# A graph-network kernel: gathered rows added by the DMA instead of VectorE, and DMA issues moved between queues

## The chip, the cores and the metric

The kernel runs on one core of a Trainium2 chip. The metric is the device time of one execution in microseconds (us). In what follows PE is the matrix engine (TensorE), DVE is VectorE, ACT is ScalarE, POOL is GpSimd, and SP is the sync engine, which only issues DMAs here. Several engines can issue DMAs: SP and ACT through hardware queues, POOL through a software queue.

## The reference

There are 12,500 nodes with 64 features each and 400,000 edges, sorted by target node `dst`. One attention-like graph layer comes first, then three message-passing layers with shared edges, with a residual and a layer norm after each of the two parts. The message-passing layer is the part that matters here:

```python
def _gnn_layer(nf, traj, src, dst, We, be, Wn, bn):
    ef = jnp.concatenate([nf[src], nf[dst], traj[:, None]], axis=-1)
    msg = jax.nn.leaky_relu(ef @ We.T + be, negative_slope=0.01)
    red = jax.ops.segment_sum(msg, dst, num_segments=nf.shape[0])
    h = jnp.concatenate([nf, red], axis=-1)
    return jax.nn.leaky_relu(h @ Wn.T + bn, negative_slope=0.01)

x = _layernorm(x + _L0_gnn_ref(x, L0_gnn_Wh, L0_gnn_weight, src, dst), axis=-1)
x = _layernorm(x + _L1_gnn_ref(x, edge_weight, src, dst, ...three layers...), axis=-1)
```

## The kernel before

`We` is split, so that the message of an edge is `leaky(A[src] + B[dst] + traj * w)`, with `A` and `B` projected once per node and layer into the tables `tabs[:, 0]` and `tabs[:, 1]`. A one-time part sorts and lays out the edges. Then the program goes through four rounds (`number` 0 to 3: the attention layer and the three message layers). Each round has a source stage, a target stage and a short dense part (`between`), and every engine waits for the end of a stage before it goes on.

**Source stage** (`source_phase`, 960 groups of 512 edges, in the order of source nodes). For each group ACT copies the table rows of one window of 128 nodes to a buffer (`window`, line 1329; the window number is loaded from `win_s` into a register). PE multiplies them with 0/1 matrices in fp8 (`hits_s`, made by DVE in round 0 and loaded by SP, line 1292, in the others), four blocks of 128 edges, three bf16 pieces each (line 1355), plus one matmul a block for the edge weight (line 1350, from `side`, line 1295; line 1352 in round 0). That is 16 matmuls a group, into one PSUM bank. DVE copies the bank to `made` (line 1378). Two groups are a lot; ACT issues the store of a lot to the table `rows` in HBM (line 1322). There are four windows, four banks, four `made` buffers; all the waits are semaphore counts (`s_window`, `s_rows`, `s_read`, `s_in`, `s_out`).

**Target stage** (`target_phase`, 976 groups, worked in 488 pairs, in the order of target nodes; rounds 1 to 3). POOL gathers 128 rows of 1 KB for each group by an indirect DMA (line 1563) into `quads`. ACT copies the window of `B` rows (line 1588); PE spreads them over the edges of the group into the PSUM bank `z` with 12 matmuls (`before_message`, line 1604; its 0/1 matrices `hits_g` come by SP, line 1573). DVE then works on a pair at a time, 512 columns on 128 partitions: `add` (line 1636: PSUM `z` plus `quads` to `msg`), `leaky` (line 1640), and `less` and `split` (lines 1644 and 1648), which cut the fp32 message into three bf16 pieces. PE sums the messages per target node (`scatter`, line 1408 in the helper `scatter_pieces`, 12 matmuls a group), two pairs behind `before_message`, and DVE adds each group's sum to `hr` (`keep`, line 1655). The order on DVE is written out for each pair `p`: `add(p)`, `less(p-1)`, `leaky(p)`, `split(p-1)`, and the two `keep` of pair `p-3`. Loops on ACT, SP and PE run in laps of 8 groups (`laps`); the lists of POOL and DVE are unrolled.

The target stage of round 0 (`first_target_phase`) gathers in the same way (line 1439) and is not touched.

Of the kernel before, what the change touches and what calls it, by code (L numbers as in the profile page):

```python
# [36 lines left out]
SLOTS = 512  # L37
# [50 lines left out]
def build(nc, x, src, dst, edge_weight, w_head, w_out, w_edge, b_edge, w_traj, w_node, b_node, out):  # L88
# [1135 lines left out]
    def laps(engine, count, step):  # L1224

        for q in range(LAP):
            step(q, q, 0)
        with engine.Fori(1, count // LAP - 1) as i:
            for q in range(LAP):
                step(i * LAP + q, q, i)  # L1230
        for g in range(count - LAP, count):
            step(g, g % LAP, g // LAP)
# [24 lines left out]
    def source_phase(number, ready, table, width):  # L1257

        layered = number > 0
        s_in, s_out = ([sem_of(f"rows_{what}{n}", layered) for n in range(4)] for what in ("in", "out"))  # L1260
        s_window, s_rows, s_read = (sem_of("rows_" + what, layered) for what in ("window", "rows", "read"))
# [4 lines left out]
        since, since_in, since_out = past * NS, past * (NS // LAP) * 32, past * (NS // LAP) * 16  # L1266
# [4 lines left out]
        window = [room.cut(3 * D // 2, BF16) for _ in range(4)]  # L1271
# [12 lines left out]
        def _(syn):  # L1284
            def load(l, n):
# [9 lines left out]
                syn.dma_start(side[0:high - low, n % 4, :, :], meta[at, low:high, :].rearrange("g r s -> r g s")).then_inc(s_in[n % 4], 16)  # L1295
# [16 lines left out]
            laps(syn, NS, step)  # L1312
            if not layered:
                store_hits(lots - 1, lots - 1)

        @block.scalar
        def _(sca):
            def store(l, n):
                if isinstance(l, int) and l < 0:
                    return  # L1320
                sca.wait_ge(s_read, since + (l + 1) * GROUP_LOT)
                sca.dma_start(to_rows[:, bass.ds(l * GROUP_LOT, GROUP_LOT), :], made[n % 4]).then_inc(s_out[n % 4], 16)
# [9 lines left out]
            for l in range(lots - 2, lots):  # L1332
                store(l, l)
# [718 lines left out]
```

## Time and profile before

| | us |
|---|---|
| median of 3 runs | 13956.04 (13951.84 to 13956.06) |
| the profiled execution, its own time | 13966.42 |
| span of the profiled execution | 13965.2 |
| source stage, round 0 | 3491 to 4555 (1064) |
| target stage, round 0 | 4590 to 5970 (1380) |
| source stages, rounds 1, 2, 3 | 955, 983, 982 |
| target stages, rounds 1, 2, 3 | 1531, 1535, 1537 |

The stage times are read from the first and last instruction of the lines that only this stage runs. The busy shares over the span are 66% for PE, 78% for DVE, 40% for ACT and 33% for POOL. These are averages over stages with different limits, so the stage tables and the waits have to be read stage by stage. In the rows further down, "PE" and "PEld" are the matmuls and the weight loads, whose ends are modelled; the number in brackets at the end of a timeline row is the idle time of the engine before it and what ended that.

### The profile page before, as it was taken

The page shows a single profiled execution, that of the slowest core. Times are in us where ns is not written, and L with a number is a line of the kernel's source. Part 1 is how long each engine was busy: PE and PEld are TensorE (multiplying, and loading weights), DVE is VectorE, ACT ScalarE, POOL GpSimd, SP SyncE. Part 2 cuts the span into 40 slices and gives each one's busy share as a digit, 9 for nine tenths or more (in the row PEclk, how much of TensorE's full clock was granted, in tenths as well). Part 3 has the DMA queues.
Part 4 walks back from the last instruction along what each step waited for, and adds up shares of the span by engine and source line. Part 5 has one row for each costly group of instructions (what it writes and reads, how often), then busy time and mean ns, then how long its engine had stood idle before and what let it go on. Part 6 is the DMA issues. An engine that isn't in the chain of part 4 may idle for free. (4 is left out here: it accounts for less than half of the span.)

```text
span 13965.2 us, 514377 instructions
## 1 busy us (share of the span) xinstructions
PE 9172.6 (66%) x172644; PEld 7604.8 (54%) x172644; DVE 10842.4 (78%) x26542; ACT 5627.0 (40%) x15578; POOL 4548.9 (33%) x4413
## 2 busy tenths in 40 slices
PE   6777777762777666667766556666555566666566
PEld 4555555541666555556655554555555555555554
DVE  8999999964777899854479996445999854479997
ACT  4666666630333688743322222333222233322222
POOL 0000000047000677610056663001666600046664
PEclk9999999965555788768899998999999989999997
DMA  1000000011788666746655555666555646665555
GB/s 34 5 5 6 5 5 6 3 25 30 238 241 241 181 197 196 172 129 207 207 180 172 172 171 98 201 201 195 171 171 171 161 123 201 201 188 171 172 172 111
DMA packets 1700459, 1931.56 MB, mean 138 GB/s; under 512 B 222450, under 2 KB 1571268, under 8 KB 1699460
## 3 DMA queue, kind: packets, MB, share of 16 engines
q1 hardware_dynamic: 977585, 893.89, 22.1%
q0 software_dynamic: 199680, 520.06, 15.1%
q10 hardware_dynamic: 522544, 510.34, 10.4%
q8 instruction: 238, 3.90, 0.1%
q14 instruction: 412, 3.38, 0.1%
HBM read 1202.74 MB, written 725.45 MB: 138 GB/s over the span
## 5 line engine op out<-in xcount | busy, mean ns | idle before, releaser
L1563 POOL DMA_INDIRECT work<-rows,quad_at x2928 | 3091.0, 1056 | 4501.8 <-DMA rows<-work 2007.4
L1378 DVE COPY work<-bank 128x256 f32<-128x256 f32 (+1 forms) x3840 | 1630.7, 425 | 1773.0 <-PE bank L1355 1748.6
L1408 PE MATMUL bank<-work 128*128 128x64 bf16 x46848 | 2077.6, 199 | 1361.4 <-DVE hr L1655 1352.2
L1355 PE MATMUL bank<-work 128*128 128x64 bf16 x46080 | 2726.2, 211 | 0.0
L1408 PEld LDWEIGHTS bank<-work 128*128 128x128 fp8e4 (+1 forms) x46848 | 1848.9, 102 | 1517.7 <-issue 1464.9
L1329 ACT COPY work<-tabs 128x192 bf16 x3840 | 1348.9, 351 | 2819.9 <-PE bank L1355 1579.4
L1588 ACT COPY work<-tabs 128x192 bf16 x2928 | 1028.9, 351 | 3548.4 <-PE bank L1604 3242.2
L1355 PEld LDWEIGHTS bank<-work 128*128 128x128 fp8e4 x46080 | 2394.1, 109 | 0.0
L1350 PE MATMUL bank<-wtraj,side 128*128 128x64 bf16 x11520 | 1772.3, 205 | 925.1 <-ACT work L1329 657.8
L521 ACT ACTIVATE work<-work,tabs 128x128 bf16<-128x128 bf16 x6250 | 1919.2, 427 | 935.0 <-DVE work L721 935.0
L1350 PEld LDWEIGHTS bank<-wtraj,side 128*128 128x128 bf16 x11520 | 1194.0, 104 | 1237.4 <-DVE work L1378 580.1
L1604 PE MATMUL bank<-work 128*128 128x64 bf16 x35136 | 1311.1, 196 | 521.1 <-DMA work<-hits_g 291.6
L1604 PEld LDWEIGHTS bank<-work 128*128 128x128 fp8e4 x35136 | 1173.8, 100 | 651.7 <-issue 600.6
L602 PE MATMUL bank<-work 128*128 128x384 bf16 x9375 | 1294.6, 292 | 40.5 <-ACT work L521 40.5
L725 DVE TENSOR_TENSOR work<-work,tabs 128x768 bf16<-128x768 bf16 x2500 | 1223.9, 552 | 0.0
L1439 POOL DMA_INDIRECT work<-rows,quad_at x976 | 986.8, 1011 | 410.1 <-issue 208.3
L1636 DVE TENSOR_TENSOR work<-bank,work 128x512 f32<-128x512 f32 x1464 | 1012.8, 692 | 129.9 <-PE bank L1604 100.4
L602 PEld LDWEIGHTS bank<-work 128*128 128x128 bf16 x9375 | 826.6, 102 | 389.0 <-issue 61.0
L1640 DVE SCALAR_TENSOR_TENSOR work<-work 128x512 f32<-128x512 f32 x1464 | 1002.8, 685 | 0.1
L1648 DVE TENSOR_TENSOR work<-work 128x512 bf16<-128x512 f32 x1464 | 1002.4, 685 | 0.1
L1644 DVE TENSOR_TENSOR work<-work 128x512 f32<-128x512 f32 x1464 | 998.1, 682 | 0.0
L1352 PE MATMUL bank<-ones_b,side 128*128 128x1 bf16 x3840 | 719.8, 190 | 411.7 <-DVE work L1370 239.4
(323 smaller groups left out, 12309.8 us busy)
## 6 DMA issues: line engine op xcount, KB each, us to landing
work<-hits_g SPq DMA_DIRECT2D x1464, 256.0 KB, 2.7
rows<-work ACTq DMA_DIRECT2D x1440, 256.0 KB, 2.1
work<-hits_s SPq DMA_DIRECT2D x1440, 128.0 KB
hits_g<-work SPq DMA_DIRECT2D x976, 128.0 KB
rows<-work ACTq DMA_DIRECT2D x480, 260.0 KB, 4.6
work<-rows,quad_at POOLq DMA_INDIRECT x3904
work<-meta_src SPq DMA_DIRECT2D x480, 128.0 KB
hits_s<-work SPq DMA_DIRECT2D x480, 128.0 KB, 4.2
```

Of the source, the lines that this page charges most:

```text
L521: last = sca.activation(values[lot % 3][:, f, j // 2, :, j % 2], of_tile(hit_col[lot % 3], j), ACT.Copy, scale=of[name][:, t:t + 1])
L602: last = ten.matmul(to[:, f * P:3 * P].rearrange("p (f c) -> p f c", c=P), of_tile(hit_row[lot % 3], j), v[:, fields[0]:fields[1], j // 2, ...
L725: last = vec.tensor_tensor(values[at][:, f, :, :, :], hit_col[at], twos(lot, name, P), ALU.mult)
L1329: sca.copy(window[q % 4].unsqueeze(1), tabs[:, 0, bass.ds(w, 1), :]).then_inc(s_window, 1)
L1350: ten.matmul(home, beside, wtraj[:, :], start=True, stop=False, skip_group_check=True)
L1355: last = ten.matmul(home, hits[n][:, q % GROUP_LOT, slots], window[q % 4][:, k * D:(k + 1) * D], start=False, stop=k == 2, skip_group_chec ...
L1378: vec.tensor_copy(made[n][:, q % GROUP_LOT, :], bank[q % 4][:, 0:QUAD * width]).then_inc(s_read, 1)
L1408: last = ten.matmul(to[:, 0:D], hits_of(j), piece_of(j), start=j == 0 and k == 0, stop=j == QUAD - 1 and k == 2, skip_group_check=True)
L1563: pool.indirect_dma_start(quads[g // 2 % (GATHERED // 2)][:, half(g)], None, table, bass.IndirectOffsetOnAxis(ap=quad_at[:, g:g + 1], axis ...
L1588: sca.copy(window[q % 4].unsqueeze(1), tabs[:, 1, bass.ds(w, 1), :]).then_inc(s_window, 1)
L1604: last = ten.matmul(to[:, j * D:(j + 1) * D], hits_t[:, j * P:(j + 1) * P], window[q % 4][:, k * D:(k + 1) * D], start=k == 0, stop=k == 2 ...
L1636: vec.tensor_tensor(msg[p % 4], z[p % 4][:, :], quads[p % (GATHERED // 2)], ALU.add).then_inc(s_added, 1)
```

## The change

In the source stage, the store of a lot goes from ACT to SP, and the load of `side` goes from SP to POOL, each lot with its own semaphore (`s_side`). There are eight windows and eight PSUM banks instead of four. This applies to all four rounds.

In the target stage, ACT copies `z` of a pair from PSUM to one of eight `msg` buffers (`hold`), one pair behind its window copies. POOL's indirect DMA no longer writes into `quads`: it adds its rows onto `msg` (`compute_op=ALU.add`). DVE's `add` is gone, and `leaky` waits for the gathers directly. `scatter` runs five pairs behind `before_message` instead of two; `hits_g` has eight buffers; the loops run in laps of 16 groups. The order on DVE becomes `leaky(p)`, `keep`, `less(p)`, `keep`, `split(p)`.

```diff
-    def laps(engine, count, step):
-        for q in range(LAP):
+    def laps(engine, count, step, size=LAP):
+        for q in range(size):
...
-        since, since_in, since_out = past * NS, past * (NS // LAP) * 32, past * (NS // LAP) * 16
+        since, since_in, since_out = past * NS, past * (NS // LAP) * 16, past * (NS // LAP) * 16
...
-        window = [room.cut(3 * D // 2, BF16) for _ in range(4)]
+        window = [room.cut(3 * D // 2, BF16) for _ in range(8)]
...
-                syn.dma_start(side[0:high - low, n % 4, :, :], meta[at, low:high, :].rearrange("g r s -> r g s")).then_inc(s_in[n % 4], 16)
+            def store(l, n):
+                if isinstance(l, int) and l < 0:
+                    return
+                syn.wait_ge(s_read, since + (l + 1) * GROUP_LOT)
+                syn.dma_start(to_rows[:, bass.ds(l * GROUP_LOT, GROUP_LOT), :], made[n % 4]).then_inc(s_out[n % 4], 16)
...
                     load(l + 3, q // GROUP_LOT + 3)
+                    store(l - 2, q // GROUP_LOT + 2)
                     if not layered:
                         store_hits(l - 1, q // GROUP_LOT + 3)
...
+        @block.gpsimd
+        def _(pool):
+            def load_side(l, n):
+                if isinstance(l, int) and l >= lots:
+                    return
+                at_least(pool, s_rows, (l - 4) * GROUP_LOT + GROUP_LOT, since)
+                pool.dma_start(side[0:high - low, n % 4, :, :], meta[bass.ds(l * GROUP_LOT, GROUP_LOT), low:high, :].rearrange(
+                    "g r s -> r g s")).then_inc(s_side[n % 4], 16)
+            def step(g, q, lap):
+                if q % GROUP_LOT == 0:
+                    load_side(lap * (LAP // GROUP_LOT) + q // GROUP_LOT + 3, q // GROUP_LOT + 3)
+            for l in range(3):
+                load_side(l, l)
+            laps(pool, NS, step)
         @block.scalar
...
             def step(g, q, lap):
-                if q % GROUP_LOT == 0:
-                    store(lap * (LAP // GROUP_LOT) + q // GROUP_LOT - 2, q // GROUP_LOT + 2)
                 w = register(sca, win_s[0:1, bass.ds(g, 1)], NW - 1)
-                at_least(sca, s_rows, g - 3, since)
-                sca.copy(window[q % 4].unsqueeze(1), tabs[:, 0, bass.ds(w, 1), :]).then_inc(s_window, 1)
+                at_least(sca, s_rows, g - 7, since)
+                sca.copy(window[q % 8].unsqueeze(1), tabs[:, 0, bass.ds(w, 1), :]).then_inc(s_window, 1)
...
-                ten.wait_ge(s_in[n], since_in + (lap + 1) * 32)
-                if not layered:
+                ten.wait_ge(s_side[n], since_in + (lap + 1) * 16)
+                if layered:
+                    ten.wait_ge(s_in[n], since_in + (lap + 1) * 16)
+                else:
                     ten.wait_ge(s_hits, g + 1)
-                at_least(ten, s_read, g - 3, since)
-                to = bank[q % 4]
+                at_least(ten, s_read, g - 7, since)
+                to = bank[q % 8]
...
+        AROUND, BEHIND = 8, 5
+        lap_groups = 2 * AROUND
         s_quads = [sem_of(f"sums_quads{n}", True) for n in range(GATHERED)]
...
-        quads = [room.cut(2 * QUAD * D) for _ in range(GATHERED // 2)]
-        hits_home = [room.cut(SLOTS, BF16).rearrange("p (g c) -> p g c", g=2) for _ in range(4)]
+        hits_home = [room.cut(SLOTS, BF16).rearrange("p (g c) -> p g c", g=2) for _ in range(AROUND)]
         window = [room.cut(3 * D // 2, BF16) for _ in range(4)]
-        msg, rest = ([room.cut(2 * QUAD * D) for _ in range(4)] for _ in range(2))
+        msg = [room.cut(2 * QUAD * D) for _ in range(AROUND)]
+        rest = [room.cut(2 * QUAD * D) for _ in range(4)]
...
             for g in range(NG):
-                at_least(pool, s_added, (g - GATHERED) // 2 + 1, since_pairs)
-                pool.indirect_dma_start(quads[g // 2 % (GATHERED // 2)][:, half(g)], None, table,
-                                        bass.IndirectOffsetOnAxis(ap=quad_at[:, g:g + 1], axis=0)).then_inc(s_quads[g % GATHERED], 16)
+                if g % 2 == 0:
+                    pool.wait_ge(s_held, since_pairs + g // 2 + 1)
+                at_least(pool, s_leaky, (g - GATHERED) // 2 + 1, since_pairs)
+                pool.indirect_dma_start(msg[g // 2 % AROUND][:, half(g)], None, table,
+                                        bass.IndirectOffsetOnAxis(ap=quad_at[:, g:g + 1], axis=0),
+                                        compute_op=ALU.add).then_inc(s_quads[g % GATHERED], 16)
...
-                at_least(syn, s_sum, 2 * (p - 3), since)
-                syn.dma_start(hits_home[n % 4], hits_g[bass.ds(p * 2, 2), :, :].rearrange("g p c -> p g c")).then_inc(s_in[n % 4], 16)
+                at_least(syn, s_sum, 2 * (p - AROUND + 1), since)
+                syn.dma_start(hits_home[n % AROUND], hits_g[bass.ds(p * 2, 2), :, :].rearrange("g p c -> p g c")).then_inc(
+                    s_in[n % AROUND], 16)
...
+            def hold(p, n):
+                sca.wait_ge(s_before, since + 2 * (p + 1))
+                at_least(sca, s_sum, 2 * (p - AROUND + 1), since)
+                sca.copy(msg[n], z[n % 4][:, :]).then_inc(s_held, 1)
             def step(g, q, lap):
                 w = register(sca, win_g[0:1, bass.ds(g, 1)], NW - 1)
                 at_least(sca, s_before, g - 3, since)
                 sca.copy(window[q % 4].unsqueeze(1), tabs[:, 1, bass.ds(w, 1), :]).then_inc(s_window, 1)
-            laps(sca, NG, step)
+                if q % 2 == 1 and (not isinstance(g, int) or g >= 2):
+                    hold(lap * AROUND + (q // 2 - 1), (q // 2 - 1) % AROUND)
+            laps(sca, NG, step, lap_groups)
+            hold(pairs - 1, (pairs - 1) % AROUND)
...
                 if q % 2 == 0:
-                    at_least(ten, s_added, lap * (LAP // 2) + (q // 2 - 3), since_pairs)
+                    at_least(ten, s_held, lap * AROUND + (q // 2 - 3), since_pairs)
                 settle(ten, "tensor", g)
-                to = z[q // 2][:, half(q)]
+                to = z[q // 2 % 4][:, half(q)]
...
-                if q % 2 == 1 and (not isinstance(g, int) or g >= 4):
-                    for h in (5, 4):
-                        scatter(g - h, (q - h) % LAP, lap - (q < h))
-            laps(ten, NG, step)
-            for g in range(NG - 4, NG):
-                scatter(g, g % LAP, g // LAP)
+                if q % 2 == 1 and (not isinstance(g, int) or g >= 2 * BEHIND):
+                    for h in (2 * BEHIND + 1, 2 * BEHIND):
+                        scatter(g - h, (q - h) % lap_groups, lap - (q < h))
...
-            def add(p):
-                vec.wait_ge(s_before, since + 2 * (p + 1))
+            def leaky(p):
                 for g in (2 * p, 2 * p + 1):
                     vec.wait_ge(s_quads[g % GATHERED], since_quads + 16 * (g // GATHERED + 1))
-                at_least(vec, s_sum, 2 * (p - 3), since)
-                vec.tensor_tensor(msg[p % 4], z[p % 4][:, :], quads[p % (GATHERED // 2)], ALU.add).then_inc(s_added, 1)
-            def leaky(p):
-                vec.wait_ge(s_added, since_pairs + p + 1)
-                vec.scalar_tensor_tensor(msg[p % 4], msg[p % 4], SLOPE, msg[p % 4], ALU.mult, ALU.max).then_inc(s_leaky, 1)
+                row = msg[p % AROUND]
+                vec.scalar_tensor_tensor(row, row, SLOPE, row, ALU.mult, ALU.max).then_inc(s_leaky, 1)
             def less(p):
                 vec.wait_ge(s_leaky, since_pairs + p + 1)
-                vec.tensor_tensor(rest[p % 4], msg[p % 4], upper(msg[p % 4]), ALU.subtract).then_inc(s_rest, 1)
+                at_least(vec, s_sum, 2 * (p - 3), since)
+                vec.tensor_tensor(rest[p % 4], msg[p % AROUND], upper(msg[p % AROUND]), ALU.subtract).then_inc(s_rest, 1)
...
             for p in range(pairs + 3):
                 if p < pairs:
-                    add(p)
-                if 1 <= p <= pairs:
-                    less(p - 1)
-                if p < pairs:
                     leaky(p)
-                if 1 <= p <= pairs:
-                    split(p - 1)
                 if p >= 3:
                     keep(2 * p - 6)
+                if p < pairs:
+                    less(p)
+                if p >= 3:
                     keep(2 * p - 5)
+                if p < pairs:
+                    split(p)
```

## Rows read from the trace of the kernel before

**Rows 1.** The page's costliest groups: the two gathers of POOL.

```profile
L1563 POOL DMA_INDIRECT work<-rows,quad_at x2928 | 3091.0, 1056 | 4501.8 <-DMA rows<-work 2007.4
...
L1439 POOL DMA_INDIRECT work<-rows,quad_at x976 | 986.8, 1011 | 410.1 <-issue 208.3
```

**Rows 2.** Busy time by stage: stretch, length, each engine, granted clock, DMA share, GB/s.

```profile
3491.00:4555.00 1064.00, 829.75 (x15360) 737.29 (x15360) 761.31 (x1919) 337.23 (x960) 0.00 (x0) 0.51 0.81 240
...
6102.00:7057.00 955.00, 691.92 (x15354) 592.53 (x15355) 407.06 (x959) 337.21 (x960) 0.00 (x0) 0.87 0.64 206
7061.00:8592.00 1531.00, 908.40 (x23424) 812.75 (x23424) 1382.32 (x2927) 342.59 (x975) 1029.49 (x976) 0.97 0.61 168
...
8706.00:9689.00 983.00, 663.33 (x15360) 556.53 (x15360) 407.29 (x959) 337.22 (x960) 0.00 (x0) 0.92 0.62 201
9693.00:11228.00 1535.00, 907.47 (x23424) 812.19 (x23424) 1382.39 (x2927) 342.98 (x976) 1030.90 (x976) 0.96 0.61 167
...
11340.00:12322.00 982.00, 661.54 (x15346) 556.27 (x15347) 406.82 (x959) 337.23 (x960) 0.00 (x0) 0.92 0.62 201
12326.00:13863.00 1537.00, 913.10 (x23424) 816.87 (x23424) 1381.92 (x2928) 342.81 (x976) 1030.62 (x976) 0.96 0.61 169
```

**Rows 3.** Timeline of DVE in the target stage of round 1, one pair: start, length.

```profile
7301.72 0.69 DVE L1636 TENSOR_TENSOR work<-bank,work 128x512 f32<-128x512 f32 x1
7302.33 0.68 DVE L1644 TENSOR_TENSOR work<-work 128x512 f32<-128x512 f32 x1
...
7304.13 0.21 DVE L1655 TENSOR_TENSOR hr<-hr,bank 128x64 f32 x1
...
7304.77 0.69 DVE L1636 TENSOR_TENSOR work<-bank,work 128x512 f32<-128x512 f32 x1
```

**Rows 4.** Timeline of POOL over the same pair.

```profile
7301.09 0.95 POOL L1563 DMA_INDIRECT work<-rows,quad_at  x1 [0.30 <-issue]
7302.68 1.16 POOL L1563 DMA_INDIRECT work<-rows,quad_at  x1 [0.64 <-DVE work L1636]
7304.14 0.96 POOL L1563 DMA_INDIRECT work<-rows,quad_at  x1 [0.30 <-issue]
```

**Rows 5.** Waits in the target stage of round 1 (7100 to 8550): total, times, longest.

```profile
POOL work L1563 <- DVE work L1636: 322.3, 467, 3.0
```

**Rows 6.** Timeline of ACT in the source stage of round 2, one lot.

```profile
9301.94 0.35 ACT L1329 COPY work<-tabs 128x192 bf16 x1 [0.85 <-PE bank L1355]
9302.74 0.35 ACT L1329 COPY work<-tabs 128x192 bf16 x1 [0.45 <-issue]
9302.97 0.38 ACTq L1322 DMA_DIRECT2D rows<-work  x1
9303.93 0.35 ACT L1329 COPY work<-tabs 128x192 bf16 x1 [0.84 <-PE bank L1355]
```

**Rows 7.** Waits of PE in the source stage of round 2 (8800 to 9600).

```profile
PE bank L1350 <- ACT work L1329: 188.6, 333, 1.1
```

**Rows 8.** Waits of SP's queue in the same stretch.

```profile
SPq L1292 <- PE bank L1355: 347.8, 390, 1.9
```

**Rows 9.** DMA queues and issues in the target stage of round 1 (7100 to 8550): share of 16 engines.

```profile
q0 software_dynamic: 44710, 122.17, 31.4%
q1 hardware_dynamic: 126741, 122.18, 29.2%
...
work<-hits_g SPq DMA_DIRECT2D x467, 256.0 KB, 2.7
work<-rows,quad_at POOLq DMA_INDIRECT x933
```

**Rows 10.** Groups of ACT by shape: a PSUM copy of 128x512 in the dense part.

```profile
L1775 ACT COPY work<-bank 128x512 f32<-128x512 f32 x72 | 41.9, 581 | 53.4 <-PE bank L1769 53.4
```

**Rows 11.** Timeline of ACT in the target stage of round 2: the second window copy of a pair.

```profile
9903.14 0.35 ACT L1588 COPY work<-tabs 128x192 bf16 x1 [0.22 <-issue]
```

**Rows 12.** Timeline of PE in the target stage of round 1: 24 matmuls early and late in it.

```profile
7072.25 1.47 PE L1604 MATMUL bank<-work 128*128 128x64 bf16 x24
...
8000.49 0.86 PE L1604 MATMUL bank<-work 128*128 128x64 bf16 x24
```

More of the change, by code:

```diff
@@ L1222, in build @@
     LAP = 8
-    def laps(engine, count, step):
-        for q in range(LAP):
+    def laps(engine, count, step, size=LAP):
+        for q in range(size):
             step(q, q, 0)
[L1228 to L1232, printed above, removed]
+        with engine.Fori(1, count // size - 1) as i:
+            for q in range(size):
+                step(i * size + q, q, i)
+        for g in range(count - size, count):
+            step(g, g % size, g // size)
     serial = itertools.count()
@@ L1260, in source_phase @@
         s_in, s_out = ([sem_of(f"rows_{what}{n}", layered) for n in range(4)] for what in ("in", "out"))
+        s_side = [sem_of(f"rows_side{n}", layered) for n in range(4)]
         s_window, s_rows, s_read = (sem_of("rows_" + what, layered) for what in ("window", "rows", "read"))
@@ L1312, in _ @@
             laps(syn, NS, step)
+            for l in range(lots - 2, lots):
+                store(l, l)
             if not layered:
                 store_hits(lots - 1, lots - 1)
+        @block.gpsimd
[12 more added lines that the diff above has]
+            laps(pool, NS, step)
         @block.scalar
         def _(sca):
[L1318 to L1322, printed above, removed]
             def step(g, q, lap):
-                if q % GROUP_LOT == 0:
-                    store(lap * (LAP // GROUP_LOT) + q // GROUP_LOT - 2, q // GROUP_LOT + 2)
                 w = register(sca, win_s[0:1, bass.ds(g, 1)], NW - 1)
-                at_least(sca, s_rows, g - 3, since)
-                sca.copy(window[q % 4].unsqueeze(1), tabs[:, 0, bass.ds(w, 1), :]).then_inc(s_window, 1)
+                at_least(sca, s_rows, g - 7, since)
+                sca.copy(window[q % 8].unsqueeze(1), tabs[:, 0, bass.ds(w, 1), :]).then_inc(s_window, 1)
             laps(sca, NS, step)
-            for l in range(lots - 2, lots):
-                store(l, l)
         @block.tensor
@@ L1354, in step @@
                     for k in range(3):
-                        last = ten.matmul(home, hits[n][:, q % GROUP_LOT, slots], window[q % 4][:, k * D:(k + 1) * D], start=False,
+                        last = ten.matmul(home, hits[n][:, q % GROUP_LOT, slots], window[q % 8][:, k * D:(k + 1) * D], start=False,
                                           stop=k == 2, skip_group_check=True)
@@ L1377, in read @@
                     at_least(vec, s_out[n], lap * 16, since_out)
-                vec.tensor_copy(made[n][:, q % GROUP_LOT, :], bank[q % 4][:, 0:QUAD * width]).then_inc(s_read, 1)
+                vec.tensor_copy(made[n][:, q % GROUP_LOT, :], bank[q % 8][:, 0:QUAD * width]).then_inc(s_read, 1)
             def step(g, q, lap):
@@ L1535, in target_phase @@
     def target_phase(number, stored, ready, table):
+        AROUND, BEHIND = 8, 5
+        lap_groups = 2 * AROUND
         s_quads = [sem_of(f"sums_quads{n}", True) for n in range(GATHERED)]
[L1538 to L1540 removed]
+        s_in = [sem_of(f"sums_in{n}", True) for n in range(AROUND)]
+        s_window, s_before, s_held, s_leaky, s_rest, s_split, s_sum, s_kept = (sem_of("sums_" + what, True) for what in (
+            "window", "before", "held", "leaky", "rest", "split", "sum", "kept"))
         past = number - 1
         pairs = NG // 2
[L1544 removed]
+        since, since_pairs, since_quads = past * NG, past * pairs, past * (NG // GATHERED) * 16
+        since_in = past * (pairs // AROUND) * 16
         room = Room(work, WORK - NG)
[L1546 to L1547 removed]
+        hits_home = [room.cut(SLOTS, BF16).rearrange("p (g c) -> p g c", g=2) for _ in range(AROUND)]
         window = [room.cut(3 * D // 2, BF16) for _ in range(4)]
[L1549 removed]
+        msg = [room.cut(2 * QUAD * D) for _ in range(AROUND)]
+        rest = [room.cut(2 * QUAD * D) for _ in range(4)]
         low = [room.cut(QUAD * D, BF16) for _ in range(4)]
```

20 lines of the change are left out of this document (10 added, 10 removed).

## The prediction

> **What bounds the kernel now.** I read the page's costliest groups first, then the busy times cut at the stage borders, and then the waits and a few microseconds of timeline inside each stage that the diff touches. The median is 13956.0; the profiled execution took 13966.4, 10 more, and its span is 13965.2. The sum below is made on the profiled execution and 10 is taken off at the end.
>
> The three layered target stages take 1531, 1535 and 1537, together 4603. DVE is busy for 1382 of each [rows 2], and its timeline shows why nothing else sets their pace: in the steady state operation follows operation. The 512-column operations start 0.60 to 0.61 apart, the two `keep` take 0.64 from the start of the first to the next `add`, and a pair repeats after 3.05 [rows 3]. Over the whole stage it is 1531/488 = 3.14 a pair, 1.03 times the steady figure, for the start and some irregular pairs. POOL gives two gathers a pair, and the first of them waits for DVE's `add` [rows 4, 5]: POOL is held back and is not the limit. PE is busy for 0.59 of the stage, the DMA engines for 0.61 [rows 2].
>
> The source stages of rounds 1 to 3 take 955, 983 and 982, or 0.995 and 1.02 a group. No engine is near full: PE 0.72 at most, ACT 0.35, DMA 0.64 [rows 2]. ACT's timeline shows a fixed beat of 2.0 a lot: 0.80 from the first window copy to the second, then a DMA issue, and the next copy 0.96 after that issue began [rows 6]. Of the 0.80, 0.35 is the copy and 0.45 is "issue", ACT's own register load and address work. PE waits for ACT's window [rows 7]. So ACT's instruction stream sets this stage, though ACT is busy for a third of it.
>
> The source stage of round 0 takes 1064, or 1.108 a group, with the DMA share at 0.81 and the PE clock at the lower of its two levels, 0.51 of 2.4 GHz [rows 2].
>
> **Target stage, part by part.** DVE loses `add` and nothing comes in its place: three operations at 0.60 and two `keep` at 0.20 is 2.20 a pair. The two `keep` used to stand side by side and the second waits for the first; in the new order a long operation lies between, so 0.20 each is what 0.64 leaves without that wait, an estimate from their length of 0.21. DVE's floor is 2.20, so another engine must take over.
>
> ACT gains one PSUM copy of 128x512, 0.58 in the dense part [rows 10]. Two window copies at 0.35+0.22 [rows 11] and the hold at 0.58+0.22 are 1.94 a pair. That is under every pace below, so it lies beside other work. If POOL and DVE both went under 1.94 it would be the price.
>
> PE does the same 48 matmuls a pair: 24 take 0.86 at the upper clock and 1.47 at the lower one [rows 12], so 1.7 or 2.94. The granted clock in these stages is 0.96 to 0.97 [rows 2], and a shorter pair leaves PE fewer idle gaps, so I take 1.7, hidden.
>
> POOL: a gather occupies it for 0.95 to 1.16 and 0.30 more lies between two [rows 4]; the mean is 1.056 [rows 1]. Nothing in this trace adds in a DMA, so its price is bounded. From below: a gather costs what it does at best, 0.96+0.30 = 1.26, a pair 2.52. From above: both sides of the transfer cost again, a busy time of 2.11, a pair 4.82. The longer gathers here are those beside DVE operations with two SBUF inputs [rows 3, 4], and in the new order three of five DVE operations are of that kind, so I don't take 1.26. With the mean, a pair is 2 x (1.056+0.30) = 2.71, and with the factor 1.03 of the present stage 2.79. I take this: the number of rows and addresses that POOL handles for one gather is unchanged. The first gather of a pair now waits for `hold` instead of `add`; behind it in POOL's queue are only later gathers, and ACT holds a pair up to four banks ahead, so this wait should be short.
>
> The Trainium skill ("GPSIMD Engine Reference", When to use GPSIMD) says that one of a pair of POOL's cores writes the read descriptors and another the write descriptors. If an adding transfer needs two reads for each row, the reading core would have twice the descriptors; that speaks against this change, and no row here shows how the 0.96 is divided. By the rule taken literally a pair would be near the 4.82.
>
> DMA engines: the gathers take 0.314 of 1450 for 933, 0.49 each of all 16 engines, and `hits_g` 0.292 of 1450 for 467, 0.91 a pair [rows 9]. A pair now asks for 1.88. An adding gather also reads 128 KB of SBUF: at nothing a pair still asks for 1.88; at double 2 x 0.98 + 0.91 = 2.87. The highest share in any row is 0.81 [rows 2], so the pace that DMA allows is 1.88/0.81 = 2.3 to 2.87/0.81 = 3.5. It reaches POOL's 2.79 when an adding gather costs 1.4 times a plain one. I take it as just hidden, between the ends.
>
> The Trainium skill ("Collectives: The Full Stack", The bandwidth ceiling) says that an adding DMA is slower because it needs two source reads on the same queue, measured at 32.35 against 62.28 GB/s, a ratio of 1.93. By that figure a pair would ask for 2 x 0.94 + 0.91 = 2.8, and 3.46 at a share of 0.81. No run so far shows it on this kernel.
>
> Depth: `scatter` five pairs behind gives a gather about four pairs, 11, for hold, queue and landing, so latency should not bind. The drain at the end is three pairs longer; with the start I add 15. A stage is 488 x 2.79 + 15 = 1377. It saves 154 + 158 + 160 = 472. Bounds: 488 x 2.52 + 15 = 1245 (saves 868) and 488 x 4.82 + 15 = 2367 (costs 2498).
>
> **Source stage, part by part.** ACT loses the store, its wait for `s_read` and its issue. What remains is the 0.80 between two copies with no DMA issue between them [rows 6]; in the target stage the same sequence takes 0.57 [rows 11], the lower bound. DMA asks for 0.62 x 1.024 = 0.64 a group, at a share of 0.81 that is 0.79. PE needs 16 x 0.86/24 = 0.57 at the upper clock and 0.98 at the lower. I take 0.80, because two independent rows meet there: 960 x 0.80 = 768. It saves 187 + 215 + 214 = 616. Bounds: DMA at full share, 0.64 or 614 (saves 1078); and nothing saved.
>
> SP gets the store (0.38 of issue [rows 6]) and loses `side`. It idles 0.89 a lot now [rows 8]. What is queued behind the new wait for `s_read` is the next lot's `hits_s` load, three lots ahead, so a short wait costs nothing; if the store came late, `made` (four buffers) would stop DVE and then PE. POOL gets the 480 `side` loads a stage; no plain DMA from POOL is in the trace, and even at the longest gather here, 1.16+0.30 [rows 4], it fits in a lot of 1.6. POOL has no other work there, so it is hidden; if it landed over three lots late, PE would stand. Eight windows and banks remove waits that are small beside ACT's beat.
>
> Round 0 asks for 0.81 x 1.108 = 0.90 of DMA a group already near the highest share, on the lower PE clock. I take 25 saved, between 100 (1.00 a group) and 40 lost, since three large DMAs of a lot now stand in SP's queue.
>
> **Sum.** 13966 - 472 - 616 - 25 = 12853, less 10 for the median: about 12845.
>
> **The rivals.**
>
> (a) The forecast: POOL paces the target stage near 2.8 and the source stage goes to 0.8. 12845, chance 0.44.
>
> (b) DMA paces the target stage, because an addition reads twice. For it: hits and gathers already take 0.61 of the engines. Against it: the 0.49 a gather may be mostly HBM latency. A pair of 2.87 to 3.53, in the middle 3.2: 488 x 3.2 + 15 = 1577, 128 more than now in three stages, with the source gain of 641 it is 13443 (ends 12950 and 13925). Chance 0.22.
>
> (c) The other side: POOL needs clearly longer to issue an adding gather. It decides from a pair of 3.55, where the three target stages lose the 641 that the source stages save: divided by 1.03, 3.45 a pair, 1.42 busy for a gather instead of 1.056. At double it is 13956 + 2498 - 641 = 15813. For it: an added read for each row is more to describe. Against it: the rows and addresses are the same in number. Chance 0.15.
>
> (d) The source stage gains nothing, since SP's store or POOL's `side` takes the place of ACT's issue, while the target stage goes as forecast: 13956 - 472 = 13484. SP's idle time speaks against it. Chance 0.13.
>
> (e) Both parts go better, 2.52 a pair and 0.72 a group (saves 868, 847, 60): 12180. Chance 0.06.
>
> **How the numbers follow.** 0.2%, 28, is about what can be told from no change. Range 12200 to 13950: it holds (a), (b), (d) and most of (e), and leaves out (c). The likeliest case alone is 12500 to 13100. Faster: 0.44 + 0.20 + 0.12 + 0.06 = 0.82; same, from the edges of (b) and (d): 0.03; slower, (c): 0.15.
>
> **What would show it.** POOL's gather row: about 1.06 says (a), over 1.4 says (c). DMA queue q0 over 0.7 a gather with POOL waiting for `leaky` says (b). ACT's two window copies at about 0.8 with no DMA issue between, and PE waiting less for ACT, show the source step; a stage still at 955 to 983, with DVE waiting for `rows` stores or PE for `side`, says (d). The prediction is wrong mainly if the addition's price, which no row shows, is far from that of a plain gather.

## The result and the profile after

The changed kernel takes 14252.2 us (median of 4 runs, 14246.3 to 14269.9) against 13955.8: the ratio is 1.0215, 95% interval 1.0197 to 1.0233. It is slower by 2.0% to 2.3%, where 8% faster was forecast, and it lies outside the range. The profiled execution has a span of 14246.8. In the sessions of three kernels further down (moved_only, side_on_pool, plain_half_rows) the kernel before itself took 15367 and 15396, with long waits inside the target stages that the profile names "remote", so of these three only ratios, differences from that kernel, the lengths of source stages and the least length of an instruction are used.

Busy time by stage in the changed kernel, with the same columns as [rows 2]:

```profile
3487.00:4537.00 1050.00, 773.24 (x15360) 707.66 (x15360) 740.57 (x1920) 337.12 (x960) 280.44 (x480) 0.57 0.85 243
6082.00:6815.00 733.00, 559.64 (x15360) 493.07 (x15360) 378.36 (x960) 337.33 (x960) 263.26 (x480) 0.99 0.87 269
6820.00:8680.00 1860.00, 1169.53 (x23424) 1065.72 (x23424) 1070.50 (x2440) 606.47 (x1464) 1549.76 (x976) 0.69 0.75 138
8793.00:9549.00 756.00, 571.92 (x15360) 498.72 (x15360) 386.27 (x960) 337.30 (x960) 263.26 (x480) 0.99 0.85 261
9553.00:11409.00 1856.00, 1155.04 (x23424) 1052.16 (x23424) 1069.97 (x2440) 622.39 (x1464) 1544.79 (x976) 0.71 0.76 138
11521.00:12273.00 752.00, 574.32 (x15360) 499.89 (x15360) 384.49 (x960) 337.34 (x960) 263.26 (x480) 0.99 0.85 262
12278.00:14145.00 1867.00, 1171.74 (x23424) 1067.14 (x23424) 1073.04 (x2439) 622.29 (x1464) 1549.26 (x976) 0.69 0.75 139
```

Two large effects of opposite sign stand in this table. The layered source stages fell from 955, 983 and 982 to 733, 756 and 752: 679 saved. Round 0 saved 14. The target stages rose from 1531, 1535 and 1537 to 1860, 1856 and 1867: 980 lost. Together that is 287 more, and the spans differ by 282.

The page's two gathers, as in [rows 1]:

```profile
L1586 POOL DMA_INDIRECT work<-rows,quad_at x2928 | 4643.8, 1586 | 944.1 <-issue 837.6
...
L1457 POOL DMA_INDIRECT work<-rows,quad_at x976 | 985.4, 1010 | 410.8 <-PE bank L1426 209.1
```

In the mean, the adding gather takes POOL 1.586 instead of 1.056, and the plain one of round 0 is unchanged at 1.01. POOL over one pair (as [rows 4]):

```profile
7301.99 1.55 POOL L1586 DMA_INDIRECT work<-rows,quad_at  x1 [0.30 <-issue]
7303.85 1.55 POOL L1586 DMA_INDIRECT work<-rows,quad_at  x1 [0.30 <-issue]
7305.70 1.55 POOL L1586 DMA_INDIRECT work<-rows,quad_at  x1 [0.30 <-issue]
```

The gathers follow each other with only the 0.30 that lies between any two. A pair takes 3.70 here and (1.586+0.30) x 2 = 3.77 in the mean, and 488 of them are 1840 of the stage's 1860. DVE in the same microseconds (as [rows 3]), and the waits of that stage from 6900 to 8600 (as [rows 5]):

```profile
7302.50 0.69 DVE L1669 SCALAR_TENSOR_TENSOR work<-work 128x512 f32<-128x512 f32 x1 [1.64 <-DMA work<-rows,quad_at]
7303.11 0.21 DVE L1685 TENSOR_TENSOR hr<-hr,bank 128x64 f32 x1
7303.24 0.68 DVE L1674 TENSOR_TENSOR work<-work 128x512 f32<-128x512 f32 x1
...
7306.10 0.69 DVE L1669 SCALAR_TENSOR_TENSOR work<-work 128x512 f32<-128x512 f32 x1 [1.44 <-DMA work<-rows,quad_at]
```

```profile
DVE work L1669 <- DMA work<-rows,quad_at: 699.7, 450, 2.7
...
POOL work L1586 <- issue: 259.2, 850, 0.3
POOL work L1586 <- DVE work L1669: 8.5, 28, 0.3
```

DVE's part went as planned and bought nothing: it is done with a pair in about 2.2 and then idles 1.4 to 1.6 for the gather, 700 of 1700. POOL waits for hardly anything: the 0.30 between its gathers adds up to 259, and DVE holds it up for 8.5. The DMA queues in that stretch (as [rows 9]):

```profile
q0 software_dynamic: 129482, 117.92, 51.3%
q1 hardware_dynamic: 122344, 117.94, 24.0%
...
work<-hits_g SPq DMA_DIRECT2D x449, 256.0 KB
work<-rows,quad_at POOLq DMA_INDIRECT x900
```

A gather now takes 0.513 x 1700/900 = 0.97 of all 16 DMA engines instead of the 0.49 of the kernel before: twice as much. A pair asks for 2 x 0.97 + 0.91 = 2.85, in a pair of 3.77.

### The profile page after: what moved, and what is told of

It reads as the page before. It is cut to its first block and busy times, and to the rows that moved or that the text cites. A ratio compares the mean times of both kernels' runs of the same rounds, so it can differ in the third digit from the quotient of the medians.

```text
span 14246.8 us, 520948 instructions
## 1 busy us (share of the span) xinstructions
PE 9551.7 (67%) x172644; PEld 8089.3 (57%) x172644; DVE 9813.9 (69%) x25078; ACT 6447.6 (45%) x17042; POOL 7167.2 (50%) x6333
## 5 line engine op out<-in xcount | busy, mean ns | idle before, releaser
L1586 POOL DMA_INDIRECT work<-rows,quad_at x2928 | 4643.8, 1586 | 944.1 <-issue 837.6
L1426 PE MATMUL bank<-work 128*128 128x64 bf16 x46848 | 2553.6, 216 | 2036.8 <-DVE hr L1685 1790.4
L1426 PEld LDWEIGHTS bank<-work 128*128 128x128 fp8e4 (+1 forms) x46848 | 2207.1, 113 | 2327.3 <-issue 2255.9
L1373 PE MATMUL bank<-work 128*128 128x64 bf16 x46080 | 2403.7, 203 | 0.0
L1613 ACT COPY work<-bank 128x512 f32<-128x512 f32 x1464 | 856.6, 585 | 3239.2 <-PE bank L1637 3238.7
L1396 DVE COPY work<-bank 128x256 f32<-128x256 f32 (+1 forms) x3840 | 1553.9, 422 | 1106.3 <-DMA rows<-work 601.7
L1331 POOL DMA_DIRECT2D side<-meta x1920 | 1070.2, 558 | 2308.3 <-PE bank L1373 2098.1
L1373 PEld LDWEIGHTS bank<-work 128*128 128x128 fp8e4 x46080 | 2156.4, 104 | 0.0
L1368 PE MATMUL bank<-wtraj,side 128*128 128x64 bf16 x11520 | 1557.5, 195 | 555.3 <-ACT work L1347 247.1
L1637 PE MATMUL bank<-work 128*128 128x64 bf16 x35136 | 1784.5, 222 | 61.4 <-DMA work<-hits_g 30.5
L1637 PEld LDWEIGHTS bank<-work 128*128 128x128 fp8e4 x35136 | 1629.0, 117 | 82.0 <-issue 50.9
L1368 PEld LDWEIGHTS bank<-wtraj,side 128*128 128x128 bf16 x11520 | 1129.3, 98 | 770.0 <-DVE work L1396 508.5
L1457 POOL DMA_INDIRECT work<-rows,quad_at x976 | 985.4, 1010 | 410.8 <-PE bank L1426 209.1
```

The lines of the kernel that those rows point to most:

```text
L1331: pool.dma_start(side[0:high - low, n % 4, :, :], meta[bass.ds(l * GROUP_LOT, GROUP_LOT), low:high, :].rearrange("g r s -> r g s")).then_i ...
L1368: ten.matmul(home, beside, wtraj[:, :], start=True, stop=False, skip_group_check=True)
L1373: last = ten.matmul(home, hits[n][:, q % GROUP_LOT, slots], window[q % 8][:, k * D:(k + 1) * D], start=False, stop=k == 2, skip_group_chec ...
L1396: vec.tensor_copy(made[n][:, q % GROUP_LOT, :], bank[q % 8][:, 0:QUAD * width]).then_inc(s_read, 1)
L1426: last = ten.matmul(to[:, 0:D], hits_of(j), piece_of(j), start=j == 0 and k == 0, stop=j == QUAD - 1 and k == 2, skip_group_check=True)
L1586: pool.indirect_dma_start(msg[g // 2 % AROUND][:, half(g)], None, table, bass.IndirectOffsetOnAxis(ap=quad_at[:, g:g + 1], axis=0), comput ...
```

## The experiments

Ratios are against the kernel before, run on the same chip in the same session; apart from the three kernels named above, it took 13956 to 13977 there.

**The two parts by themselves.** tgt_only has the source stage of before and the target stage of after; src_only the reverse (each function taken whole, so the diff is the one half or the other of the change).

> Source stages as before, target stages as in the changed kernel. Theory (POOL pays for the adding gather, nothing else of the loss comes from elsewhere): source stages back to 955 to 983, target stages 1855 to 1867, so about 13956 + 979 = 14935. Rival (the two parts disturb each other, for instance through the clock or the buffers): off this sum by more than 60.

> Target stages as before, source stages as in the changed kernel. Theory (the two parts are independent): the three layered source stages save 682 and round 0 saves 15, so about 13260. Rival (the target stage profits or suffers from a changed source stage): off by more than 60.

Measured: tgt_only 14946.8, ratio 1.0707 (1.0689 to 1.0725); src_only 13259.7, ratio 0.9500 (0.9484 to 0.9516), both within 12 of the expected sums. The parts are independent: one saves 697 (5%), the other costs 990 (7%).

**The price of adding.** no_add takes the addition out and leaves every wait, copy and buffer of the changed kernel.

```diff
-                                        bass.IndirectOffsetOnAxis(ap=quad_at[:, g:g + 1], axis=0),
-                                        compute_op=ALU.add).then_inc(s_quads[g % GATHERED], 16)
+                                        bass.IndirectOffsetOnAxis(ap=quad_at[:, g:g + 1], axis=0)).then_inc(s_quads[g % GATHERED], 16)
```

> The changed kernel with plain gathers, which overwrite what ACT copied, so the B part of the messages is left out of the result; every wait and instruction else is the same. Theory (the time is the price of adding in POOL's issue, 1.55 against 0.96 to 1.16): a gather back at about 1.06, a pair at 2.71 to 2.8, target stages 1330 to 1380, so about 12800. DMA theory: the gather's DMA time back from 0.97 to 0.49 with the same effect, so this run alone does not part them. Rival (the new order of waits sets the pace: hold, leaky, keep): target stages stay over 1600.

Measured: 12930.2, ratio 0.9263 (0.9248 to 0.9279). One argument is worth 1322. POOL's gather in its target stage of round 1, 6900 to 8000, and the DMA queue of the gathers there:

```profile
L1586 POOL DMA_INDIRECT work<-rows,quad_at x782 | 862.9, 1103 | 238.3 <-issue 183.7 <-DVE work L1668 29.6 <-ACT work L1612 25.0
```

```profile
q0 software_dynamic: 37509, 102.50, 28.3%
```

POOL still paces the stage: (1.103+0.30) x 2 = 2.81 a pair, and 1100/391 is 2.81. The mean gather is 1.10 where 1.06 was expected, which is some 40 a stage, and the target stages take 1423, 1419 and 1429 instead of 1330 to 1380: that makes the 130 by which this run lies over the expected 12800. With target stages over 100 shorter than those of the kernel before, the new order of waits is fast enough, and the whole loss is the addition's.

**POOL or the DMA engines.** add_half_bytes keeps 128 rows a gather and halves the bytes; add_half_rows takes 64 rows.

```diff
-                pool.indirect_dma_start(msg[g // 2 % AROUND][:, half(g)], None, table,
+                pool.indirect_dma_start(msg[g // 2 % AROUND][:, half(g)][:, 0:QUAD * D // 2], None, table.rearrange("r (h c) -> (r h) c", h=2),
```

```diff
-                pool.indirect_dma_start(msg[g // 2 % AROUND][:, half(g)], None, table,
-                                        bass.IndirectOffsetOnAxis(ap=quad_at[:, g:g + 1], axis=0),
+                pool.indirect_dma_start(msg[g // 2 % AROUND][0:64, half(g)], None, table,
+                                        bass.IndirectOffsetOnAxis(ap=quad_at[0:64, g:g + 1], axis=0),
```

> The changed kernel, where every adding gather takes 128 rows of 512 B instead of 1 KB (the other half of each message is left as ACT copied it, and the rows are other ones, so the messages are not the reference's). Rows and descriptors are as many, the bytes are half. Theory (POOL pays for each row it describes): the gather on POOL stays at 1.55 and the pair at 3.75, about 14250, while the DMA time of a gather falls well below 0.97. Rival (POOL or the stage is held back by the DMA engines' added traffic): POOL's gather or the pair gets shorter, by up to 0.8 a pair, below 13900.

> The changed kernel, where every adding gather takes 64 rows instead of 128 (partitions 64 to 127 of a message are left as ACT copied them, so half of the source rows are missing from the result). Theory (a fixed part and a price for each row): the gather on POOL falls clearly, to 0.8 to 1.1, and the stage is then set by DVE at 2.2 to 2.4 a pair, target stages 1080 to 1200, about 12200 to 12500. Rival (the price of adding is a fixed one for each instruction): the gather stays over 1.3 and the stages over 1550.

Measured: add_half_bytes 14502.9, ratio 1.0376 (1.0346 to 1.0406); add_half_rows 14263.1, ratio 1.0204 (1.0175 to 1.0234). The DMA queue of the gathers from 6900 to 8600, first with half the bytes, then with half the rows (865 and 897 gathers):

```profile
q0 software_dynamic: 124477, 56.71, 27.7%
```

```profile
q0 software_dynamic: 71713, 58.80, 24.7%
```

With half the bytes the DMA time of a gather fell to 0.277 x 1700/865 = 0.54, and with half the rows to 0.247 x 1700/897 = 0.47, and neither kernel is faster than the changed one. So the DMA engines' doubled work, though real, does not set the pace; POOL's own time does. Both times missed what was expected: the first is 250 over its 14250, though POOL's median gather stays at 1.55 as expected, and the second is far above 12200 to 12500, since 64 rows hardly help POOL (its rival, a fixed price, named over 1.3 for the gather and over 1550 for the stage, and that is what came). To see what is left without the addition, plain_half_rows is no_add with the 64 rows.

> The changed kernel with plain gathers of 64 rows (no addition; the B part is overwritten in partitions 0 to 63 and half of the source rows are missing, so the messages are not the reference's). With 128 rows a plain gather took POOL 0.95 at least and an adding one 1.54; with 64 rows an adding one took 1.41. Theory (adding costs POOL a fixed 0.59 for each instruction, whatever the rows): 1.41 less 0.59, about 0.82, and the stage goes to DVE's and POOL's pace of 2.3 to 2.5 a pair, about 12400 to 12600. Rival (the price grows with the rows, and another part does not): the least gather is off 0.82 by more than 0.1.

Its time was 14427.3, ratio 0.9365 (0.9338 to 0.9392), beside the kernel before at 15396; the 12400 to 12600 that were expected can't be judged from it. The gather's line in four kernels (least, median and longest, ns): the changed kernel, add_half_rows, no_add, plain_half_rows.

```profile
L1586 POOL DMA_INDIRECT work<-rows,quad_at x2928: 1538/1547/2074, 6824.7 to 14135.4; - x196
```

```profile
L1586 POOL DMA_INDIRECT work<-rows,quad_at x2928: 1405/1442/1936, 6857.7 to 14155.0; - x196
```

```profile
L1586 POOL DMA_INDIRECT work<-rows,quad_at x2928: 951/1052/1487, 6822.5 to 12819.5; - x196
```

```profile
L1586 POOL DMA_INDIRECT work<-rows,quad_at x2928: 909/962/1427, 7187.8 to 14326.7; - x196
```

By the least durations, adding costs POOL 0.59 with 128 rows and 0.50 with 64. Half of the rows save 0.13 with the addition and 0.04 without. A straight line through the two would put about 0.4 of the 0.59 on the instruction and 0.2 on its 128 rows (an estimate from these four numbers, and two row counts are few for a line). My theory of a wholly fixed 0.59 asked for 0.82 with 64 plain rows and got 0.91: mostly fixed, not wholly.

Why is add_half_bytes slower than the changed kernel, by some 225 by the ratios? Its timeline, POOL and then DVE:

```profile
7300.97 1.74 POOL L1586 DMA_INDIRECT work<-rows,quad_at  x1 [0.30 <-issue]
7303.01 1.55 POOL L1586 DMA_INDIRECT work<-rows,quad_at  x1 [0.30 <-issue]
7304.86 1.92 POOL L1586 DMA_INDIRECT work<-rows,quad_at  x1 [0.30 <-issue]
```

```profile
7300.59 0.69 DVE L1669 SCALAR_TENSOR_TENSOR work<-work 128x512 f32<-128x512 f32 x1 [1.74 <-DMA work<-rows,quad_at]
...
7304.66 0.69 DVE L1669 SCALAR_TENSOR_TENSOR work<-work 128x512 f32<-128x512 f32 x1 [1.91 <-DMA work<-rows,quad_at]
```

Both long gathers begin inside `leaky`: the first 0.31 before its end and 0.19 longer than 1.55, the second 0.49 before its end and 0.37 longer. The gather at 7303.01 begins with DVE idle and takes 1.55. Since `leaky` starts when a gather has landed, and the next gather starts a fixed time after the last, a changed landing time shifts one against the other, and the shorter transfer shifts it the wrong way: the mean gather is 1.662, and 0.076 more for 2928 gathers is 223, the whole difference.

The traces bear this out over all 2928 gathers of each kernel. A gather that begins while DVE works on two SBUF inputs is longer than the least one by the time left of that operation less about 0.12. With 0.3 to 0.4 left it is longer by 0.23 in the median (changed kernel and add_half_bytes), with over 0.6 left by 0.5, and with under 0.1 left by nothing. Nearly all others are within 0.02 of the least. In the changed kernel 1279 gathers begin so, and they are 0.10 longer in the mean; in add_half_bytes it is 1555 and 0.22, in add_half_rows 1571 and 0.32. So add_half_rows did make the gather 0.13 shorter at its least, and lost all of it to this phase: its mean gather is 1.583, that of the changed kernel 1.586. What shifts the phase in each kernel is read from timelines; no run was made for it alone.

**Which move helps the source stage.** Three kernels have the source stage's moves singly or without the wider buffers, with the target stage of before.

store_on_sp: in the source stage only the store goes from ACT to SP (the added line stands in SP's step behind its load, the removed ones stood in ACT's step; `store` itself moves with them).

```diff
+                    store(l - 2, q // GROUP_LOT + 2)
...
-                if q % GROUP_LOT == 0:
-                    store(lap * (LAP // GROUP_LOT) + q // GROUP_LOT - 2, q // GROUP_LOT + 2)
```

> The kernel before, where only the store of a lot moves from ACT to SP; side stays on SP, four windows and four banks stay. Theory (ACT's instruction stream sets the source stages of rounds 1 to 3, and the store is what makes it long): nearly the whole gain of 682 comes from this alone, 13300 to 13450. Rival (the eight windows and banks bring it): under 200 saved.

Measured: 13836.4, ratio 0.9899 (0.9870 to 0.9928): 141 of the 697 that src_only saves. Most is missing, and the expected 13300 to 13450 were not reached. Its layered source stages take 892, 928 and 895, which is 205 less than before, but that of round 0 takes 1140 instead of 1064. SP's queue in its source stage of round 2:

```profile
9201.69 0.34 SPq L1292 DMA_DIRECT2D work<-hits_s  x1
9202.23 0.30 SPq L1295 DMA_DIRECT2D side<-meta  x1
9202.79 0.41 SPq L1301 DMA_DIRECT2D rows<-work  x1
9203.51 0.34 SPq L1292 DMA_DIRECT2D work<-hits_s  x1
```

SP issues DMAs without a wait, three in 1.82, which is 0.91 a group; before, ACT's beat was 2.0 a lot [rows 6] and SP idled 0.89 of it [rows 8]. The store filled that idle time, and SP became the limit. In round 0 SP also stores `hits_s`, four issues a lot, and by their median distances they take 2.30, or 1104 of the 1140.

eight_only: only the windows and PSUM banks of the source stage go from four to eight.

```diff
-        window = [room.cut(3 * D // 2, BF16) for _ in range(4)]
+        window = [room.cut(3 * D // 2, BF16) for _ in range(8)]
...
-                at_least(ten, s_read, g - 3, since)
-                to = bank[q % 4]
+                at_least(ten, s_read, g - 7, since)
+                to = bank[q % 8]
```

> The kernel before, where only the windows and PSUM banks of the source stage go from four to eight; both DMA issues stay where they were. Theory (ACT's stream sets the stage): nothing, 13900 to 13956. Rival (the wait for PSUM and windows sets it): 300 or more saved.

Measured: 14004.7, ratio 1.0020 (1.0008 to 1.0031), 27 more than the kernel before on that chip. Nothing gained, if anything a little lost.

side_on_pool: only the load of `side` moves, to POOL. moved_only: both moves, four windows and banks.

> The kernel before, where only the load of side moves from SP to POOL; the store stays on ACT, four windows and banks stay. The store alone on SP saved 1% because SP then issued three DMAs a lot, 1.8 apart. Theory (two queues each carry one issue too many for a stage of 0.76 a group: ACT 2.0 a lot with the store, SP 1.8 with three): ACT's stream still sets the stage, so nothing is saved here, 13900 to 13990. Rival (SP's queue was the limit all along and ACT's beat is only its image): 300 or more saved.

> The kernel before with both DMA issues moved (store to SP, side to POOL) and four windows and banks. With the store alone on SP and with all parts together (13260) known, this parts the rest: if side on POOL is worth something, this lies at 13260 and the store alone above it; if the eight windows and banks are, this lies above 13260 by what they bring. I expect 13260 to 13350.

Measured: side_on_pool 1.0003 (0.9991 to 1.0014), with layered source stages of about 961, 990 and 990; moved_only 0.9550 (0.9513 to 0.9587), with 730, 754 and 747, the lengths of the changed kernel. It took 685 less than the kernel before beside it, and src_only 697 less. Store alone 1%, side alone nothing, both nearly everything: ACT's stream ends at 2.0 a lot, SP's with three issues at 1.8, and only when both are relieved does the stage come to 1.5. The wider buffers add nothing that these runs can tell.

**A version that beats both.** keeps_apart takes the new source stage, the old target stage, and of the new order on DVE only that the two `keep` of a pair don't stand side by side. In the kernel before, the second waits 0.22 for the first (the pair of [rows 3]):

```profile
7304.57 0.22 DVE L1655 TENSOR_TENSOR hr<-hr,bank 128x64 f32 x1 [0.22 <-DVE hr L1655]
```

```diff
                 if p < pairs:
                     add(p)
+                if p >= 3:
+                    keep(2 * p - 6)
                 if 1 <= p <= pairs:
                     less(p - 1)
                 if p < pairs:
                     leaky(p)
+                if p >= 3:
+                    keep(2 * p - 5)
                 if 1 <= p <= pairs:
                     split(p - 1)
-                if p >= 3:
-                    keep(2 * p - 6)
-                    keep(2 * p - 5)
```

> The new source stages and the old target stage, of which only DVE's order is changed: one keep after add, the other after leaky. Theory (DVE's stream sets the old target stage, the second keep waits about 0.22 to 0.24 for the first): a pair 3.05 to 2.82 in the steady state, 488 x 0.23 = 112 less a stage, about 12925. POOL's floor of 2.71 is close. Rival (PE's sums then come late for the first keep, since it stands two operations earlier): no gain or a loss against the same kernel with the old order (about 13260).

Measured: 12821.9, ratio 0.9187 (0.9172 to 0.9202), 438 under src_only and 1430 under the changed kernel. DVE and POOL over one pair of it:

```profile
7302.70 0.69 DVE L1654 TENSOR_TENSOR work<-bank,work 128x512 f32<-128x512 f32 x1
7303.31 0.21 DVE L1673 TENSOR_TENSOR hr<-hr,bank 128x64 f32 x1
7303.44 0.68 DVE L1662 TENSOR_TENSOR work<-work 128x512 f32<-128x512 f32 x1
...
7305.48 0.69 DVE L1654 TENSOR_TENSOR work<-bank,work 128x512 f32<-128x512 f32 x1
```

```profile
7302.57 1.03 POOL L1581 DMA_INDIRECT work<-rows,quad_at  x1 [0.31 <-issue]
7303.91 1.04 POOL L1581 DMA_INDIRECT work<-rows,quad_at  x1 [0.30 <-issue]
7305.25 1.03 POOL L1581 DMA_INDIRECT work<-rows,quad_at  x1 [0.30 <-issue]
```

A pair takes 2.78 on DVE here (2.74 in the mean of 402), and 2.68 on POOL: they meet. It gained 0.07 a pair more than I expected (438 over 1464 pairs is 0.30, and 0.23 was expected); the timeline shows a `keep` delay the long operation behind it by 0.13, not by the 0.20 that I had counted. Taking `leaky` from DVE to ACT as well, or two groups in one gather, was not tried; by these rows the first would leave POOL's 2.68 as the limit.

## Why the prediction was wrong

**The step that failed** is the price of an adding gather on POOL: "I take this: the number of rows and addresses that POOL handles for one gather is unchanged." The sum took 1.056; it is 1.586. That makes a pair 3.77 instead of 2.71 (2.79 with the factor of 1.03) and a stage 1860 instead of 1377, three times 483, which is 1449 and more than the whole miss of 1407. The reason given for it does not hold: the rows were indeed as many, and the price came all the same, because about 0.4 of the 0.59 sits on the instruction and only 0.2 on its rows (the estimate from add_half_rows and plain_half_rows). No row of before shows an adding DMA, and I took a point near the lower end of 2.52 to 4.82 as the likeliest. The measured 3.77 is in the middle of it.

**Rival (c) is what happened.** It had the place right, POOL's issue of the adding gather, and the point from which it decides, 1.42 busy; 1.586 lies beyond it. With 1.586 its arithmetic gives 488 x 3.77 + 15 = 1855, against 1860, 1856 and 1867; with the factor of 1.03, which it also took, it would be 1910, and a stage that POOL alone paces did not need it. Its chance of 0.15 was too small, and the range, which left it out, was too short at the upper end for a cost without a row.

The Trainium skill ("GPSIMD Engine Reference", When to use GPSIMD), that one core writes read descriptors and another the write descriptors, pointed to the right engine. Twice the read descriptors, as the prediction drew from it, would make the price of adding fall to half with 64 rows, from 0.59 to about 0.3 (an estimate); it fell to 0.50, so the runs do not bear out that reading.

**Rival (b)**: its premise was right and its conclusion not. The DMA time of a gather doubled, 0.49 to 0.97, and a pair asks for 2.85. But POOL issues a pair only every 3.77, so the DMA engines stand at 0.75, and halving their work gained nothing. The Trainium skill ("Collectives: The Full Stack", The bandwidth ceiling) gives 1.93 for the two reads of an addition, measured between two collective operations. Here the trace shows 0.97/0.49 = 1.98 against the kernel before, which agrees, and 0.97/0.40 = 2.4 against no_add, where a plain gather takes 0.283 x 1100/782 = 0.40: the addition at least doubles the DMA time, and how much more depends on the plain gather that it is held against. A faster POOL would have met this limit next: 2.85 at the share of 0.87 seen in the source stage is 3.3 a pair, still over the old 3.14. That last figure is an estimate and was not run.

**The rest of the target stage** held. DVE's floor was put at 2.20 and its work on a pair takes about 2.2; `hold` takes 0.58 as forecast; no_add, the forecast's case without the price of adding, has a steady pair of 2.81 where 2.71 was written before the factor of 1.03 and 2.79 with it, stages of 1419 to 1429 where 1377 was, and a total of 12930 where 12845 was. The granted clock in these stages fell from 0.96 to 0.97 in the kernel before to 0.69 to 0.71, with PE busy for 0.63 of the stage and waiting for DVE's `keep` in most of the rest; in no_add it is 0.99. That was not foreseen, and since POOL waits for hardly anything, it is not what holds the stage back.

**The source stage** held in its number, a little better: 616 forecast, 679 measured, at 0.76 to 0.79 a group where 0.80 was taken, and a DMA share of 0.85 to 0.87 where 0.81 was the highest seen. The reason held in part. That ACT's issue had to go was right, but the 0.80 between ACT's copies was not the next pace: ACT now waits for PE, and DVE waits for stores to land (source stage of round 2, 8850 to 9500):

```profile
ACT work L1347 <- PE bank L1373: 263.3, 513, 1.2
...
DVE work L1396 <- DMA rows<-work: 150.1, 205, 1.6
```

So the closeness of 0.80 to the measured pace is in part luck. Which of PE, DVE's chain and the DMA engines sets the new pace, no run parts.

That eight windows and banks add nothing was right. What I had underrated is `side`: I wrote of SP's idle 0.89 a lot as enough. It was so only because `side` left the queue; store_on_sp shows what happens without that. Round 0: 25 forecast, 14 measured.

**The sum**: 13966 - 472 - 616 - 25 was written; with the measured terms it is 13966 + 980 - 679 - 14 = 14253.

## What to carry to other kernels

Before giving an operation to an engine that merely has idle time, price that engine's instruction in its new form; if no trace shows it, a run of the one instruction is worth more than a point chosen in a wide range, and the range has to keep its far end. Work saved on the limiting engine is worth only the way down to the next limit: here 0.85 a pair came off DVE (3.05 to 2.20), and POOL, 0.43 below the old pace of 3.14, was made 1.06 a pair longer at the same time. When DMA issues move between queues, count the issues of every queue a lot, since an issue costs SP's queue 0.54 to 0.72 here, for 18 KB as for 128 and 256 KB. And put short operations that depend on each other between long ones: that reordering alone gave 438 here.

## What the runs showed of the hardware

- An indirect gather with addition takes POOL 1.54 at least, a plain one 0.95 (128 rows of 1 KB; after and no_add); with 64 rows 1.41 and 0.91 (add_half_rows, plain_half_rows). Half the bytes did not change the least length: with 512 B rows it is also 1.54 (add_half_bytes).
- A gather with addition takes 0.97 of all 16 DMA engines, a plain one 0.49 (before) or 0.40 (no_add), one with addition and 512 B rows 0.54 (add_half_bytes).
- A gather that begins while DVE works on two SBUF inputs is longer by what is left of that operation less about 0.12, up to 0.53, as if it waited for that operation's end. One that begins at another time is hardly longer (0.01 in the mean of 1600 in the changed kernel), even when such an operation starts in the middle of it. The Trainium skill ("SBUF — State Buffer", Who interferes with whom) says that a VectorE instruction with two SBUF inputs contends with a GpSimd instruction that reads SBUF; these traces agree with that, for the start of a gather.
- SP issues DMAs one after another every 0.54 to 0.72 in the layered source stages of store_on_sp, although each is shown as 0.30 to 0.41 long.
